# The accumulating transfer issued behind the low half, and maxima spread by a stationary block with stride zero

## The reference, cut to what matters

```python
x = x + attn(cond(x, cond_128, ...), Wq, Wk, Wv, Wo, q_norm_w, k_norm_w)      # x: 32 x 32 x 512
f = cond2(x, cond_128, ...)                          # a mixed 1x1 convolution, 32 x 32 x 512
gate = silu(f @ gate_proj)                           # 512 -> 1792
up = f @ up_proj                                     # 512 -> 1792
x = x + (gate * up) @ down_proj                      # 1792 -> 512
```

## Time and profile before

| | |
|---|---|
| median of 3 runs | 681.24 us (680.61 to 681.83) |
| the profiled execution | 680.94 us |
| its span, from the first to the last instruction | 679.1 us |
| PE busy | 659.5 us, 97% |
| DVE busy | 563.2 us, 83% |
| POOL busy | 458.5 us, 68% |
| ACT busy | 411.9 us, 61% |
| accumulating transfers | 24 of 512 KB, from 535.7 to 665.5 us |

### The profile page before, as it was taken

How to read it: one execution, slowest core, us unless ns; L and a number is a source line. 1 busy time by engine, 2 the same in 40 slices (tenths; PEclk the granted TensorE clock), 3 DMA queues, 4 the chain that set the end, 5 groups by cost and what they waited for, 6 DMA issues and landing times.

```text
span 679.1 us, 14435 instructions
## 1 busy us (share of the span) xinstructions
PE 659.5 (97%) x4952; PEld 370.0 (54%) x4952; DVE 563.2 (83%) x870; ACT 411.9 (61%) x1233; POOL 458.5 (68%) x379
## 2 busy tenths in 40 slices
PE   9998999999999999999999999999989999999995
PEld 8855555646566465665656656565644434444441
DVE  4979779879879788987978888777785999899997
ACT  0477663845647384374655638446475778877874
POOL 0367973884685497288659648747537678887886
PEclk9999999999999999999999999999999999999998
DMA  7520157379359348536735943563300156556454
GB/s 262 189 95 1 66 163 140 94 178 183 104 100 270 94 90 268 104 89 158 203 85 106 278 109 77 160 106 102 57 1 0 32 109 124 110 110 139 94 105 113
DMA packets 112672, 82.70 MB, mean 122 GB/s; under 512 B 93264, under 2 KB 93936, under 8 KB 110448
## 3 DMA queue, kind: packets, MB, share of 16 engines
q1 hardware_dynamic: 108736, 69.51, 40.4%
q0 software_dynamic: 3456, 12.58, 9.9%
q10 hardware_dynamic: 432, 0.01, 0.0%
HBM read 48.14 MB, written 2.21 MB: 74 GB/s over the span
## 4 chain that ended last, share of the span: by engine, by line
PE 75%; DVE 8%; POOL 7%; issue 4%; DMA 3%; ACT 2%; SPq 1%; POOLq 0%; DVEq 0%; ACTq 0%
PE bank L677 19%; PE bank L679 18%; PE bank L678 18%; PE bank L1053 2%; PE bank L1054 2%; PE bank L1037 2%; PE bank L1061 2%; PE bank L1038 2%; PE bank L1057 2%; DMA acc<-dprod 2%; POOL wqlo L2156 2%; PE bank L877 1%; DMA wqr<-in_wq 1%; DVE mx L1594 1%; DVE exact L2032 1%
## 5 line engine op out<-in xcount | busy, mean ns | idle before, releaser
L677 PE MATMUL bank<-wohi,oThi 128*128 128x512 f16 x256 | 97.1, 379 | 2.2 <-DVE oTlo L1802 2.1
L677 PE MATMUL bank<-wqhi,cThi 128*128 128x512 f16 x256 | 97.0, 379 | 0.8 <-POOL wqlo L2156 0.6
L678 PE MATMUL bank<-wolo,oThi 128*128 128x512 f16 x256 | 97.0, 379 | 0.0
L679 PE MATMUL bank<-wohi,oTlo 128*128 128x512 f16 x256 | 97.0, 379 | 0.0
L679 PE MATMUL bank<-wqhi,cTlo 128*128 128x512 f16 x256 | 97.0, 379 | 0.0
L678 PE MATMUL bank<-wqlo,cThi 128*128 128x512 f16 x256 | 97.0, 379 | 0.0
L1222 ACT ACTIVATE qraw<-bank 128x512 f32<-128x512 f32 x64 | 37.9, 592 | 82.4 <-PE bank L679 82.1
L2166 POOL TENSOR_TENSOR wolo<-wor,wohi 128x512 f16<-128x512 f32 x32 | 42.6, 1353 | 57.9 <-ACT wohi L1202 57.9
L2204 POOL TENSOR_TENSOR qinv<-qms,neghalf 128x8 f32<-128x8 f32 x28 | 53.6, 1914 | 39.3 <-ACT qms L1241 39.3
L1233 ACT ACTIVATE qsq<-qraw 128x128 f32<-128x128 f32 x256 | 75.5, 302 | 1.7
L677 PE MATMUL bank<-wkvhi,cThi 128*128 128x256 f16 x256 | 69.9, 273 | 0.0
(11 more groups left out here) (231 smaller groups left out, 1806.6 us busy)
## 6 DMA issues: line engine op xcount, KB each, us to landing
acc<-dprod POOLq DMA_DIRECT2D x24, 512.0 KB, 4.6
wqr<-in_wq SPq DMA_DIRECT2D x8, 1024.0 KB, 7.4
wor<-in_wo SPq DMA_DIRECT2D x8, 1024.0 KB, 9.2
raw<-in_gu_w SPq DMA_DIRECT2D x28, 256.0 KB, 3.5
zeros<-in_gu_z SPq DMA_DIRECT2D x28, 256.0 KB, 4.6
wkvr<-in_wkv SPq DMA_DIRECT2D x8, 512.0 KB, 7.2
raw<-in_dn_w SPq DMA_DIRECT2D x14, 256.0 KB, 2.8
zeros<-in_dn_z SPq DMA_DIRECT2D x14, 256.0 KB, 3.5
```

What stands on the lines that cost most here:

```text
L677: mm(o, ahi, bhi, start=start and k == 0, stop=False)
L678: mm(o, ahi, blo, start=False, stop=False)
L679: last = mm(o, alo, bhi, start=False, stop=stop and k == n - 1)
```

## The change

GpSimd's queue: `move_down(n - 3)` now stands behind `hidden_low(n - 1)` instead of between `hidden(n - 1)` and `add_part(n)`, for n = 3 to 26; for n = 27 it stays where it was. In tiles 8 and 10 it stands ahead of the tiny products. Its waits are the same.

The maxima: VectorE no longer makes the diagonal. TensorE multiplies the identity of 4 (as moving operand) with the column of four maxima read 128 times (stride zero, as weights). The constant block had 1/`TOP` and the diagonal `TOP` in it, and both are gone. For the second half the reduction has one more wait, on the first half's matmul, long past by then.

```diff
             def hidden_all(half):
-                pe.wait_ge(d_hdiag, half + 1)
+                pe.wait_ge(d_hrow, half + 1)
                 if half == 0:
                     pe.wait_ge(d_fup, 1)
-                mm(bound_all(), spread[0:MAXIMA, :], hdiag[0:MAXIMA, :], start=True, stop=True).then_inc(t_hx, 1)
+                mm(bound_all(), hrow[0:MAXIMA, :].broadcast_to([MAXIMA, P]), ident[0:MAXIMA, 0:MAXIMA],
+                   start=True, stop=True).then_inc(t_hx, 1)
...
-            def hidden_diagonal(half):
+            def hidden_maxima(half):
                 dve.wait_ge(t_hx, 2 * half + 1)
-                link(V.tensor_reduce(hrow[0:MAXIMA, :], bound_rows(half), AX_X, ALU.max))
-                V.scalar_tensor_tensor(hdiag[0:MAXIMA, :], ident[0:MAXIMA, 0:MAXIMA], TOP,
-                                       hrow[0:MAXIMA, :].broadcast_to([MAXIMA, MAXIMA]), ALU.mult,
-                                       ALU.mult).then_inc(d_hdiag, 1)
+                if half:
+                    dve.wait_ge(t_hx, 2)
+                V.tensor_reduce(hrow[0:MAXIMA, :], bound_rows(half), AX_X, ALU.max).then_inc(d_hrow, 1)
...
             for n in range(LAG, TILES):
                 if n > LAG:
                     hidden(n - 1)
+                if n == TILES - 1:
                     move_down(n - 1 - LAG)
                 add_part(n)
                 hidden_low(n - 1)
+                if LAG < n < TILES - 1:
+                    move_down(n - 1 - LAG)
                 if n == 8:
                     hidden_product(1)
                 elif n == 10:
```

More of the change, by code:

```diff
@@ L408, in build @@
         d_hx = sem("d_hx")
-        d_hdiag = sem("d_hdiag")
+        d_hrow = sem("d_hrow")
         t_hx = sem("t_hx")
@@ L2078, in _ @@
             mix_power(0)
-            hidden_diagonal(0)
+            hidden_maxima(0)
             probs_low(UNITS - 1)
@@ L2102, in _ @@
                 elif n == 6:
-                    hidden_diagonal(1)
+                    hidden_maxima(1)
                 elif n == 9:
```

## The result

The changed kernel took 686.55 us (median of 6 runs, 685.53 to 689.05) against 681.34 for the kernel before in the same session: a ratio of 1.0066, 95% interval 1.0042 to 1.0090. That is 4.5 us slower by the ratio and 5.2 by the medians; the forecast was 683.6, its range ended at 685.5. The direction was right, the size was not. The profiled execution took 687.15 us, span 685.3, against 680.94 and 679.1.

The account below looks back on a forecast made before the run. TensorE was taken as the bound, with transfers about 5 us apart against tiles of 5.1 to 5.2. Terms summed to +2.4 us on 680.94, so 683.3, plus 0.3 for the median: 683.6 us, range 681.1 to 685.5.

Parts of the forecast that it names:

- Diagonal, first half: VectorE's chain in the first half loses the diagonal instruction: 0.15 us gained (0 to 0.3).
- Diagonal, second half: Tile 6: without VectorE's diagonal, held beside GpSimd's multiply, gate pass and waiting matmul come earlier: 0.9 us gained (0 to 1.05).
- Tiles 8 and 9: Scale products behind the moved issue lose 0.2 to 0.6 us, against 0.2 gained at another wait; taken as +0.2.
- Wait for the low half at tile 13: TensorE's stop for GpSimd's low half goes, 1.16 us, and 0.19 in the next block: 1.35 us gained.
- the last transpose, which I take at 0: Behind tile 13: with the transfer 2.6 us later it may land earlier or later; 0 (0.5 gained to 2 lost).
- Loss A: Tiles 16 and 17: transfer 13 lands later, VectorE's result(1) and then TensorE wait: 2.4 us lost (2.3 to 4.3).
- a lower clock for the tail alone: TensorE's pause of 2 us in the tail brings the lower clock; last matmuls cost 1 us more.
- Loss B: Tail: transfer 23 issued later, so transfer 24 waits and everything to the end shifts: 2.2 us lost (1.7 to 4.1).
- the issue of transfer 23: End of tile 26: issued at 662.7 us once the low half ends, landing at 667.3.
- Quiet tiles: Tiles where TensorE is full: nothing gained from moving the transfer, 0.
- more is lost: Late transpose at tile 14, lower clock in the tail, or diagonal's 0.9 not gained: +1 to +2 more, 685.1 us; chance 0.15.
- The rival of a shorter landing: Transfers land sooner than the trace says, both losses shrink; at 3.2 us landing the kernel takes 680.8 us; chance 0.07.

Follow-up runs that it names:

- e2: The kernel before with only the transfers moved behind the low half, the diagonal kept: 689.20 us, ratio 1.0100.
- e4: The kernel before with transfer 23 alone moved behind the low half, in tile 26: 683.88 us, ratio 1.0031.
- e10: e7 with the transfers behind the low half only up to tile 15, ahead of the adds from tile 16 on: 683.16 us, ratio 1.0010.
- e11: Second run of the kernel before with only the maxima changed, no transfer moved: 680.59 us, ratio 0.9984.
- e1: The kernel before with only the maxima changed (stride-zero weights, no diagonal), no transfer moved: 680.52 us, ratio 0.9988.
- e6: The changed kernel with TensorE turning the third column of x behind the up matmuls in tile 17: 684.54 us, ratio 1.0033.
- e7: e6 with VectorE's result(1) behind the eviction and sum of tile 17, result(2) behind the up eviction: 684.34 us, ratio 1.0037.
- e9: The changed kernel with 17 more pairs of weight load and one-column matmul on TensorE ahead of tile 17's transposes: 685.85 us, ratio 1.0058.

## Why the prediction was wrong

By its own steps, the term and then what the table says:

- **Diagonal, first half, -0.15.** Not measurable: the gate of tile 5 stands between 537.3 and 539.8 us in the 13 profiles, whichever kernel. The head of +0.49 in the pair goes with the granted clock of 0.50 behind 500 us: with it tiles 0 to 4 took 0.6 us longer, and it came in kernels of either form.
- **Diagonal, second half, -0.9.** Right: -0.96. VectorE's instruction with SBUF operands stood until GpSimd's multiply ended; in e2, with all else moved, it took 0.92 us again, and the reduction from PSUM in its place takes 0.27 inside the same multiply. The Trainium skill, "SBUF — State Buffer", section "SBUF: two separate sides", says that the first kind is locked out by GpSimd; the trace agrees, and that the second is not held is seen in the 0.27.
- **Tiles 8 and 9, +0.2.** +0.05 in tiles 7 to 12. Nearly nothing, as in the sum.
- **Wait for the low half at tile 13, -1.35.** The wait went, and the step from the gate of tile 14 to that of 15 fell by 1.79 us (6.98 to 5.19), more than forecast; but the step before it grew by 1.15 (5.23 to 6.38), and tiles 12 to 16 gained 0.63. The step that failed is "the last transpose, which I take at 0": TensorE stood 1.04 us for it, within the bounds that stood beside it. The wait was 0.9 to 1.04 us in the eight profiles with the transfers behind the low half up to there, and between none and 0.57 in the five others. What makes this transpose land later I didn't test.
- **Loss A, +2.4.** The mechanism right to the idle: 2.46 us forecast as 2.4, 2.5 us at the full clock. Mis-sized by leaving the granted clock out of the sum. I had weighed a lower clock for the tail alone, and at +1; it came behind this stop, in four of the seven profiles with a stop of 2 us or more, and cost up to 1.6 (16.59 against 15.02).
- **Loss B, +2.2.** 2.2 by itself (e4), 3.52 in the changed kernel. The step that failed is the issue of transfer 23, which I set by the end of the low half (662.7, on the clock of before). With all transfers behind the low half, GpSimd reaches each issue only 0.1 us after the chain of landings allows it. One late landing then delays all the later issues: 23 was issued after an idle of 0.97 us, for a landing. In the kernel before, the chain is as tight, but a late landing holds the sum and the low half, so TensorE stands for it and pays at once: one tile of 5.9 us in e4, e10 and e11, behind a landing of 5.1. Behind the low half it is not felt until the end.
- **Quiet tiles, 0.** -0.34 from 18 to 27.

The terms that were mis-sized are the clock (+1.6), the carried lateness (+1.3) and the wait at tiles 13 and 14 (+0.7). The head adds 0.6, which is not the change's, and the other terms take 0.5 back; that is the 3.8 us, to a tenth, between the forecast of 2.4 and the 6.2 of the profile. The rival "more is lost" was given 0.15. It had the last transpose in its list, and the lower clock at the wrong place: in the tail of the profile after the clock did fall to 0.50, from 674.1 to 680.8 us, with 5.7 us of TensorE's work in it, but the end stands 13.6 us behind the last issue, as before. The rival of a shorter landing fell: 24 transfers, none under 4.5 us, with or without the transposes beside them. The Trainium skill, "DMA: Bandwidth & Descriptors", section "Anatomy of one DMA — SWDGE (gpsimd) path", gives an estimate of 3.2 us for it; the trace disagrees in all 13 profiles.

The best of the versions is the maxima alone (e1, e11), likely about 1 us faster than before. The move didn't pay in any form that I ran: its gain is about 1 us in tiles 12 to 16 (22.2 to 22.4 against 23.0 to 23.75), and at its cheapest, in e10, its debt cost 2.7 in tiles 16 and 17 (15.18 against 12.49).

## What to carry to other kernels

When a serial chain (here transfers that wait for each other, 5.07 us apart) runs nearly as slowly as the loop (5.18 us), moving its link later in an iteration is a debt that isn't paid back in the iterations that follow; look for each reader of a landing with less cover than the shift, and for the place where the link moves back. And add to such a sum what one late landing does, since a chain without slack hands it on to the end. A stop of TensorE is to be priced with the chance of the lower clock behind it, not by its own length.

## What the hardware did that I had not expected

- A fetch of 0.02 MB of instructions in the middle of a 512 KB accumulating transfer delayed its landing from 4.5 to about 6 us; near its end it cost 0 to 0.6 after 625 us. In the transfer issued at 633.98 (after), 5 of its 144 packets start later than 4.5 us behind the issue; in the one issued at 628.80, without a fetch, none does.
- Around the same stop of TensorE of about 2.7 us, the granted clock fell to 0.50 for 3.4 us in one profile of the changed kernel and stayed at 1.00 in the other; TensorE was busy for 3.2 us of these, of which half, 1.6, is an estimate of the price; the table says 1.57. With idles of 1 us or less (e6, e7) it stayed at 1.00.
- 17 one-column matmuls with their weight loads took 0.57 us on TensorE (e9).
